# One table of token sums instead of two: every accumulating scatter waits for the one before it, and the last stage loads one row per token

## The reference, cut to what matters

```python
logits = xf @ gate_inp.T
topv, topi = jax.lax.top_k(logits, K)                  # K = 4
w = jax.nn.softmax(topv, axis=-1)
dense_w = zeros((n, E)).at[arange(n)[:, None], topi].set(w)
u = einsum('nc,ehc->neh', xf, W_up)
g = einsum('nc,ehc->neh', xf, W_gate)
h = silu(g) * u
y = einsum('neh,ech,ne->nc', h, W_down, dense_w)
...
x = _layernorm(x + y)
```

## Time and profile before

| | us |
|---|---|
| median of 3 runs (2379.24 to 2386.84) | 2381.57 |
| the profiled execution | 2376.07 |
| its span, first to last instruction | 2374.3 |
| first gather of the experts block starts at | 1614.00 |
| last scatter starts at | 2322.05 |
| first load of the combine block starts at | 2332.33 |

### The profile page before, as it was taken

One profiled execution on the slowest core, in us unless ns is written; L12 is line 12 of the kernel. 1 busy time (PEld: TensorE's weight loads), 2 busy tenths in 40 slices (PEclk: granted clock), 3 DMA queues, 4 the chain that ended last, 5 costly groups with the idle time before them and its releaser, 6 DMA issues. The chain is left out here.

```text
span 2374.3 us, 35555 instructions
## 1 busy us (share of the span) xinstructions
PE 2004.2 (84%) x9744; PEld 1382.1 (58%) x9745; DVE 1387.9 (58%) x2699; ACT 725.5 (31%) x1473; POOL 1135.4 (48%) x903
## 2 busy tenths in 40 slices
PE   4599989989989989999899898722899999999990
PEld 2366656656656657666566565521566666666760
DVE  4676786776776776767866867231344444444445
ACT  2224334233233333243343342200222222222323
POOL 3353553554554554545545545121455555555654
PEclk8799999999999999999999999865999999999995
DMA  6111111111111111111111011029433333333437
GB/s 228 36 44 46 50 36 46 56 28 53 39 38 57 43 38 57 36 45 49 35 46 56 28 49 45 1 71 280 97 59 55 57 58 54 58 57 58 62 54 221
DMA packets 141647, 149.94 MB, mean 63 GB/s; under 512 B 36320, under 2 KB 131744, under 8 KB 141216
## 3 DMA queue, kind: packets, MB, share of 16 engines
q1 hardware_dynamic: 101152, 85.11, 12.3%
q0 software_dynamic: 31744, 38.04, 10.2%
q10 hardware_dynamic: 8704, 26.22, 3.8%
HBM read 89.96 MB, written 59.34 MB: 63 GB/s over the span
## 5 line engine op out<-in xcount | busy, mean ns | idle before, releaser
L991 POOL TENSOR_TENSOR y<-y,v 128x1024 f32<-128x1024 f32 (+1 forms) x128 | 330.5, 2582 | 164.6 <-DVE v L1139 159.8
L1443 PE MATMUL pu<-w_ug,xh 128*128 x1728 | 353.3, 354 | 24.4 <-DVE xh L1554 12.6
L1563 DVE TENSOR_TENSOR gate_hid<-pu,gate_hid 128x448 f32<-128x448 f32 x144 | 90.0, 625 | 363.3 <-ACT gate_hid L1507 360.9
L730 PE MATMUL pb<-x1T,w_sw 128*128 128x256 f32 x1024 | 276.5, 426 | 13.3 <-ACT x1T L834 11.0
L1599 POOL DMA_INDIRECT xin<-x_dram,meta_in x144 | 140.9, 978 | 306.2 <-PE px L1427 176.2
L1443 PEld LDWEIGHTS pu<-w_ug,xh 128*128 128x128 bf16 x1728 | 167.9, 98 | 175.2 <-issue 47.3
L730 PEld LDWEIGHTS pb<-x1T,w_sw 128*128 128x128 f32 x1024 | 218.7, 217 | 86.6 <-issue 21.8
L1609 POOL DMA_INDIRECT sums_dram<-yo,meta_in x144 | 228.0, 1583 | 61.2 <-issue 42.4
L1507 ACT ACTIVATE gate_hid<-pu 128x448 f32<-128x448 f32 x144 | 78.4, 544 | 470.1 <-PE pu L1443 470.1
L1469 PE MATMUL py<-w_dn,hh 112*128 x1728 | 213.6, 273 | 7.8 <-issue 3.8
L625 PE MATMUL pa<-u,masked 128*128 128x512 f32 x448 | 209.1, 601 | 11.6 <-DVE u L1129 6.5
(11 more groups left out here) (224 smaller groups left out, 3406.8 us busy)
## 6 DMA issues: line engine op xcount, KB each, us to landing
w_stage<-in_w_ug SPq DMA_DIRECT2D x64, 224.0 KB, 2.8
split_ug<-w_parts SPq DMA_DIRECT2D x64, 224.0 KB, 2.5
w_ug<-split_ug ACTq DMA_DIRECT2D x16, 896.0 KB, 28.9
rows<-sums_dram SPq DMA_DIRECT2D x32, 256.0 KB, 5.5
w_stage<-in_w_dn SPq DMA_DIRECT2D x32, 224.0 KB, 2.9
split_dn<-w_parts SPq DMA_DIRECT2D x32, 224.0 KB, 2.8
w_dn<-split_dn ACTq DMA_DIRECT2D x16, 448.0 KB, 30.2
xT<-in_xT SPq DMA_DIRECT2D x16, 256.0 KB, 2.7
```

Source lines behind the costliest of these rows:

```text
L730: last = mm(pb[:, 1 + j % 2, w * T:(w + 1) * T], w_sw[:, c, o:o + P], x1T[:, c, :], start=c == 0, stop=c == DC - 1)
L991: nc.gpsimd.tensor_tensor(y[:, first:NT, :], y[:, first:NT, :], v[:, k % 2, first:NT, :], ALU.add).then_inc(y_added.sem, 1)
L1443: last = mm(pu[:, 2 * b + w, 0:EH], xh[:, b, xp, c, :], w_ug[:, bass.ds(e, 1), wp, c, w * EH:(w + 1) * EH], start=n == 0, stop=n == 3 * DC ...
```

## The change

There is one table. It starts as x3, nothing is zeroed but its 128 rows for padding. Every scatter goes to it, and so each waits, beside `y_ready`, for the landing of the scatter one tile back. The combine block loads one row per token and has no sum; statistics and the final scaling read the loaded rows themselves, so that a slot of `rows` is free only when ACT has normalised it.

```diff
-    sums_dram = [nc.dram_tensor(f"sums_dram{n}", [ntok + P, D], F32).ap() for n in range(2)]
+    sums_dram = nc.dram_tensor("sums_dram", [ntok + P, D], F32).ap()
...
-        nothing = sb("nothing", [P, NT * D])
+        nothing = sb("nothing", [P, D])
...
-                    for sums in sums_dram:
-                        sp.dma_start(sums[nseq * T:nseq * T + P, :], nothing[:, 0:D]).then_inc(sums_cleared.sem, 16)
+                    sp.dma_start(sums_dram[nseq * T:nseq * T + P, :], nothing[:, :]).then_inc(sums_cleared.sem, 16)
...
-                for to, rows in ((x3_dram, x3), (sums_dram[0], x3)):
+                for to, rows in ((x3_dram, x3), (sums_dram, x3)):
...
-                sp.dma_start(sums_dram[1][bass.ds(s * T, T), :].rearrange("(t p) d -> p t d", p=P),
-                             nothing[:, :].rearrange("p (t d) -> p t d", d=D)).then_inc(x3_stored.sem, 16)
...
                 pool.wait_ge(y_ready.sem, y_ready.at(i))
+                if later(i):
+                    pool.wait_ge(y_stored[(m - 1) % 2].sem, y_stored[(m - 1) % 2].at(UN // 2 * r + (m + 1) // 2 - 1))
                 carrier.take()
                 nc.gpsimd.indirect_dma_start(
-                    out=sums_dram[m % 2], out_offset=bass.IndirectOffsetOnAxis(ap=meta[:, m, 0:1], axis=0),
+                    out=sums_dram, out_offset=bass.IndirectOffsetOnAxis(ap=meta[:, m, 0:1], axis=0),
                     in_=yo[:, m % 2, :], in_offset=None, compute_op=ALU.add
                 ).then_inc(y_stored[m % 2].sem, 16)
...
-        rows = sb("rows", [P, CS, 2, NT, D])
-        res = sb("res", [P, CS, NT, D])
-        st = sb("st", [P, NT, 6])
+        rows = sb("rows", [P, CS, NT, D])
+        st = sb("st", [P, CS, NT, 6])
...
                 if later(i, CS):
-                    sp.wait_ge(summed.sem, summed.at(i - CS))
-                for n, sums in enumerate(sums_dram):
-                    sp.dma_start(rows[:, m, n, :, :], sums[bass.ds(i * T, T), :].rearrange("(t p) d -> p t d", p=P)
-                                 ).then_inc(loaded[m].sem, 16)
+                    sp.wait_ge(normed.sem, normed.at(i - CS))
+                sp.dma_start(rows[:, m, :, :], sums_dram[bass.ds(i * T, T), :].rearrange("(t p) d -> p t d", p=P)
+                             ).then_inc(loaded[m].sem, 16)
...
-                vec.tensor_tensor(res[:, m, :, :], rows[:, m, 0, :, :], rows[:, m, 1, :, :], ALU.add
-                                  ).then_inc(summed.sem, 1)
-                dve.wait_ge(summed.sem, summed.at(i))
-                for t in range(NT):
-                    last = vec.bn_stats(st[:, t, :], res[:, m, t, :])
+                for t in range(NT):
+                    last = vec.bn_stats(st[:, m, t, :], rows[:, m, t, :])
...
-                    last = nc.scalar.activation(fin[:, m, t, :], res[:, m, t, :], ACT.Identity, scale=mv[:, m, t, 1:2],
+                    last = nc.scalar.activation(fin[:, m, t, :], rows[:, m, t, :], ACT.Identity, scale=mv[:, m, t, 1:2],
```

More of the change, by code:

```diff
@@ L369, in layers_block @@
         nothing_set = sig("nothing_set", 1)
-        sums_cleared = sig("sums_cleared", 16 * 2)
+        sums_cleared = sig("sums_cleared", 16)
         padding_stored = sig("padding_stored", 16 * (NE + 1))
@@ L455, in layers_block @@
         meta_ready = sig("meta_ready", 1)
-        x3_stored = sig("x3_stored", 16 * 3)
+        x3_stored = sig("x3_stored", 16 * 2)
         meta_stored = sig("meta_stored", 16 * NT * TOPK)
@@ L1640, in combine_block @@
         fin = sb("fin", [P, CS, NT, D])
-        loaded = [sig(f"loaded{n}", 32) for n in range(CS)]
-        summed = sig("summed", 1)
+        loaded = [sig(f"loaded{n}", 16) for n in range(CS)]
         norm_step = sig("norm_step", 1)
@@ L1695, in _, with statistics @@
             carrier = Carrier(dve, waited)
-            def sums(i, m, r):
+            def statistics(i, m, r):
                 chain.start(i)
@@ L1709, in sums @@
                 for t in range(NT):
-                    last = vec.bn_aggr(mv[:, m, t, :], st[:, t, :])
+                    last = vec.bn_aggr(mv[:, m, t, :], st[:, m, t, :])
                 last.then_inc(variance_ready.sem, 1)
@@ L1719, in step @@
             def step(i, m, r):
-                sums(i, m, r)
+                statistics(i, m, r)
                 if later(i):
```

## The result

The changed kernel takes 2391.78 us in the median of 20 runs (2383.96 to 2399.57). The kernel before, in 20 runs beside it, takes 2379.65 (2346.36 to 2392.76). The ratio is 1.0085, with an interval of 1.0057 to 1.0113: slower by 0.85%. That lies inside the range of the prediction (2368 to 2398), but not in its forecast, which was no change that can be told; slower had a chance of 0.38.

The account below looks back on a forecast made before the run. A POOL, SP and DMA chain was taken to bound most of the experts block, PE some 25 tiles. 2376.07 + 8.0 - 3 = 2381.1, plus half of 5.5, gave 2384 us; forecast's own range 2376 to 2392, overall 2368 to 2398.

Parts of the forecast that it names:

- What bounds before: Experts block: a POOL, SP and DMA chain, 9.3 us per two tiles, for most of it; PE for some 25 tiles.
- The new wait: Experts block: each scatter waits for the last one's landing, 3.81 + 0.80 = 4.61 us per scatter; block +8.0 us.
- Scatter 3: Start of the experts block: this scatter moves from 1683.17 to 1684.7, 4.7 us after scatter 2 at 1680.00.
- The last block: Combine block: slots held until ACT is done, landing 3.3 us, ring 5.9 us per three sequences; 38.8 us, -3 us.
- The sum: Whole kernel: 2376.07 + 8.0 - 3 = 2381.1 us on the profiled execution.
- From the profile to the median: Whole kernel: the profiled sum lies 5.5 us below the median of the runs; half is taken, giving 2384 us.
- Edits at nothing: Layers block: removed zero stores, one clearing store and half a memset are covered by PE's work; 0, bounds -5.5 to 0.
- slower period: Experts block rival: accumulates on the table just written, or a slower release, give 4.78 us per scatter; 2408 us, chance 0.15.
- slot ring with a landing of 5.5: Last block rival: loads land as slowly as now, 9 us over the sum, 2393 us; chance 0.13.
- hidden wait: Experts block rival: POOL's sequencer uses the time before the landing, so the block stays as it is; 2376 us, chance 0.10.
- faster period: Experts block rival: a scatter alone lands in 3.65 us, period 4.45, -22 us; 2362 us, chance 0.07.
- block that follows its bytes: Last block rival: time follows 8.4 of 12.6 MB, 28 us, -14 us; 2373 us, chance 0.05.

Follow-up runs that it names:

- 8-slot runs: Changed kernel with eight instead of four slots in the last block, run twice: 2376.26 us (0.9998 to before) and 2383.02 us (1.0085 to before).
- one-load kernel: Kernel before with the changed kernel's last block, loading only the first table and leaving the second table's sums out: 2378.72 us, 0.9996 to before.
- three groups: Follow-up kernels, each group run on one chip beside the kernel before, whose medians were 2380.24, 2380.87 and 2369.78 us.
- group 3: Kernels run on one chip beside the kernel before (2369.78 us), among them the changed kernel again, unaltered: 2389.86 us, 1.0101 to before.
- wait-alone run: Kernel before, two tables and old last block, with only the changed kernel's new wait added: 2389.87 us, 1.0044 to before.

## Why the prediction was wrong, step by step

The step that failed is the size of the term for the experts block, **+8.0 us** in the prediction: measured are +16.2 (2338.23 - 2322.05), because the interval of the scatters is 4.661 us and not 4.61. The landing in the last block was mis-sized too, by which -3 became -0.9. Neither is a wrong mechanism, and together they carry the forecast from "no change" to slower.

**What bounds before** was right; 16 record buffers give PE-bound scatters 4.2 apart and 60 us.

**The new wait** was right in its mechanism and mis-sized in its term. Even scatters, record loads of 1.6 us, the gather fitting between, PE idle for (445 - 419.71) / 95 = 0.27 us per tile in that stretch (0.4 forecast; the modelled ends of PE make this coarse): all seen. The term was 4.61 per scatter; measured are 4.661 (4.675, 4.685, 4.689, 4.650, 4.672 in the other kernels with this ring). 140 x 0.051 = 7.2 us. About half is the ring itself: without the five long intervals the mean is 4.635, 0.03 over the 3.81 + 0.80 that I took from two rows. The other half, 3.7 us, is what those five are over the median. Before, POOL stood idle for 3.3 us in every second tile; a delay could vanish there. For two of the tiles its trace shows that hardly any is left: where the ring's intervals are 6.04 and 5.45 (after tiles 52 and 71), those of before are 3.18 and 6.35, beside the usual 3.2 and 6.1 to 6.2. Tiles 52 and 53 before:

```profile
1915.03 1.59 POOL L1609 DMA_INDIRECT sums_dram<-yo,meta_in  x1 [0.30 <-issue]
1916.92 0.98 POOL L1599 DMA_INDIRECT xin<-x_dram,meta_in  x1 [0.30 <-issue]
1918.21 1.58 POOL L1609 DMA_INDIRECT sums_dram<-yo,meta_in  x1 [0.31 <-issue]
```

Whether the delay was absorbed there or did not arise, the trace cannot tell. The prediction had no term for such delays. The upper bound, 4.78, held. An error of 1% in a period was as large as the term: +8 was the small difference of two larger numbers, as the text said, and its bounds (4.45 to 4.78, 46 us) were wider than the forecast's own range allowed for.

The Trainium skill (DMA: Bandwidth & Descriptors, Anatomy of one DMA) gives 2.0 us plus bytes over 436 GB/s, for a scatter an estimate of 2.3 us. It counts the setup in its 2.0, so 2.3 alone does not fit the landing measured here, 3.84 us after the start (the mean of the two releases above). It fits what is left of the 3.84 behind the 1.58 us of the instruction, 2.26. The prediction's 3.9 is such a sum of the page's figure and a row.

With 3.9 the prediction had a period of 4.7, and with the rows of before 4.61; the measured 4.661 lies between them, almost in the middle. Without the five long intervals the mean is 4.635, nearer to 4.61. So the trace does not decide for the page's estimate.

**Scatter 3** came at 1685.64 instead of 1684.7, because scatter 2 came 1.0 later.

**The last block** was right in its mechanism, with one main size off: the loads land in 4.0 us, not 3.3, which by the prediction's own sum makes a ring of 6.6 and a block of 7.0 + 4 x 6.6 + 3 x 1.8 + 2.8 = 41.6; measured 41.1. Of the -3 remained -0.9. With eight slots, where this ring is gone, the block takes 33.8 to 34.0 (36.8 forecast for that case), though the loads land no sooner (4.1 and 4.2). There ACT's own pace is 1.66 us per sequence and not the 1.8 that the prediction read while the DMA was full, and that alone is 2 us. So 7 us of gain are lost to the four slots, as the 8-slot runs show. Why the loads take 4.0 is open: the stores of ACT, as large and as slow (4.0), run beside them, but no run separates them.

**The sum**, as a span: 2374.3 + 8.0 - 3 = 2379.3 forecast, 2390.0 measured. The miss of 10.7 us is 0.9 (scatter 3) + 7.2 (period) + 0.4 (last scatter to first load) + 2.3 (last block) = 10.8, up to rounding. All four have the same sign: nothing cancelled.

**From the profile to the median** I added half of 5.5 us, for the case that before's fast rhythm was longer in its profiled execution than usual. That was nearly right in size: between the profiles the change costs 15.8 us (2391.86 - 2376.07), between the medians 12.1, which is 3.7 less, where I had taken off 2.7. The two rhythms fit this: the profile of before, with some 25 even intervals, is of an execution 3.6 us faster than the median of 20, and the one-load kernel's, with three loosened ones, of one 8.8 slower than its median. Two profiles do not prove it. The medians of before were 2380, 2381 and 2370 in the three groups, with single runs down to 2344; after spans 2384 to 2400 only, with medians of 2392 and 2390. The loss by the change is therefore 12 us in the first comparison and 20 in group 3: the base moved and the changed kernel hardly did.

**Edits at nothing:** the layers block ended (first record load) 0.9 us later than before, within the 10 us by which it moves between executions. Nothing gained, nothing lost that can be told.

**The rivals.** The slower period (2408) was the right direction, at a third of its size: the period rose by 0.05, not by 0.17. It was not the table just written, as the wait-alone run shows, and the release was hardly slower (0.79 and 0.85 instead of 0.80). The slot ring with a landing of 5.5 did not come, but its point of decision, 4.8, was nearly reached by single loads (4.7). The hidden wait, the faster period and the block that follows its bytes are refuted: the wait alone costs 9.6 us against before on the same chip; no kernel with the wait has a mean interval below 4.64; half the loads gave 1.5 us, not 14. Against a faster period the prediction held that the landing is the same in both stretches of the earlier trace rows; those rows show no landing, but the trace does, and it is so: a scatter of the fast stretch starts at 2200.96 and has landed at 2204.8 by SP's release, 3.84 us later.

## What to carry to other kernels

A wait on one's own predecessor turns a loose sequence into a ring whose period is landing plus release; if that lies near the present average, expect to lose: here the old average still held slack that absorbed delays and let PE run at its own pace for stretches, and the ring held none. Before trading buffers or tables for traffic, look for the ring that binds now: here more buffers for 2 KB record loads brought 60 us, and with the new ring they brought nothing. When a slot's owner changes from a short first user to the last user, count the ring anew with the landing under the traffic that remains, and add slots if it is above the engine's pace.

## What the runs showed of the hardware that was not expected

- The 0.8 us between a landing and the start of POOL's indirect DMA is not the engine's time. A memset of 0.53 us fitted into it for 0.08 us per scatter; one of 0.95 us cost 0.44.
- The same experts block runs in two rhythms, in pairs (3.2 and 6.2 us) or evenly (4.2), and how long each holds differs between executions: some 25 even intervals in one profile, three loosened ones in another, and the last scatter 13 us apart (3 us of it from the start of the block). A single profile of such a kernel is good to some 10 us.
- Single intervals between scatters grow by 0.3 to 1.4 us with nothing in the profile that explains them (2.1 us from release to start at 1917.0 to 1919.12). They are tied to the tile and not to chance: the intervals after tiles 52, 71 and 107 are long in all twelve traces in which the scatters stand evenly throughout (eight with the new wait, four with 16 record buffers and two tables). With slack they are made up in the next interval (5.49, then 3.17), without it they stay. What causes them is open.
